# Row dots with the mask term as their seed, single-row matmuls and a mask in five parts, in a recommender's attention kernel

## The reference, cut to what matters

```python
maskf = hist_mask.astype(dt)
decay = jnp.exp(-(softplus(decay_alpha) + 1e-6) * hist_age_hours) * maskf
mean_hist = (hist_items * maskf[..., None]).sum(1) / (maskf.sum(1, keepdims=True) + 1e-06)
q = mean_hist @ Wq.T
k, v = hist_items @ Wk.T, hist_items @ Wv.T                 # (512, 200, 128)
scores = einsum('bd,btd->bt', q, k) * scale + jnp.log(decay + 1e-12)
scores = jnp.where(hist_mask, scores, -jnp.inf)
attn = softmax(scores); long_term = einsum('bt,btd->bd', attn, v)
# short_term: mean of five items; g: sigmoid gate of mean popularity and age
user = g * short_term + (1 - g) * long_term
out = layernorm(user) * ln_gamma + ln_beta                  # (512, 128)
```

## Time and profile before

| | |
|---|---|
| time, median of 3 runs | 208.8 us (206.55 to 209.44) |
| time of the profiled execution | 206.09 us |
| its span, first to last instruction | 204.4 us |
| mean granted TensorE clock | 0.946 |
| busy: TensorE, VectorE, ScalarE, GpSimd | 168.8, 174.1, 118.8, 143.0 us |
| moved from and to memory | 55.19 MB, 270 GB/s |

### The profile page before, as it was taken

One profiled execution on the slowest core, in us unless ns is written; L12 is line 12 of the kernel. 1 busy time (PEld: TensorE's weight loads), 2 busy tenths in 40 slices (PEclk: granted clock), 3 DMA queues, 4 the chain that ended last, 5 costly groups with the idle time before them and its releaser, 6 DMA issues.

```text
span 204.4 us, 6882 instructions
## 1 busy us (share of the span) xinstructions
PE 168.8 (83%) x2005; PEld 102.9 (50%) x2005; DVE 174.1 (85%) x1332; ACT 118.8 (58%) x646; POOL 143.0 (70%) x167
## 2 busy tenths in 40 slices
PE   0172864887999699899999999999999999997890
PEld 0132432444565456565655565656565656564570
DVE  0513989989999999999899999898999998989703
ACT  2002255587767377667676777676677776768410
POOL 3467982488959587777869887769698877486311
PEclk9998555699999999999999999999999999999998
DMA  7949969996888878988988899988888998600000
GB/s 36 303 153 304 257 223 420 418 431 287 311 293 326 325 268 287 339 328 277 333 311 331 345 330 338 321 318 323 311 328 287 386 363 313 246 2 14 0 3 13
DMA packets 15683, 55.19 MB, mean 270 GB/s; under 512 B 10160, under 2 KB 11312, under 8 KB 11568
## 3 DMA queue, kind: packets, MB, share of 16 engines
q1 hardware_dynamic: 15088, 53.64, 74.2%
q0 software_dynamic: 576, 1.33, 2.2%
HBM read 54.70 MB, written 0.26 MB: 269 GB/s over the span
## 4 chain that ended last, share of the span: by engine, by line
POOL 31%; issue 25%; PE 17%; DVE 14%; DMA 8%; ACT 3%; POOLq 1%; ACTq 0%; SPq 0%; DVEq 0%
POOL gprod L286 14%; DVE junk_v L686 9%; PE ps_sum L358 6%; POOL mblk L266 6%; DMA x<-in_r_hist_items_dram 5%; POOL pblk L275 5%; PE ps_wx L358 4%; DMA mask_p<-in_r_hist_mask_dram 3%; PE ps_sum L368 3%; PE ps_query L377 2%; POOL pop_taken L344 2%; POOL age_taken L344 2%; ACT sums L467 1%; POOL taken L322 1%; PE ps_group L386 1%
## 5 line engine op out<-in xcount | busy, mean ns | idle before, releaser
L686 DVE SCALAR_TENSOR_TENSOR junk_v<-x,ps_query 128x128 f32<-128x128 f32 x576 | 127.2, 277 | 7.5 <-ACT query L485 7.3
L286 POOL TENSOR_TENSOR gprod<-x,query 128x512 f32<-128x512 f32 x64 | 71.9, 1144 | 32.0 <-ACT query L485 31.9
L458 ACT ACTIVATE gprod<-gprod 128x128 f32<-128x128 f32 x224 | 66.1, 299 | 2.7 <-DVE kept L653 1.4
L358 PE MATMUL ps_wx<-x,pblk 128*32 128x256 f32 (+1 forms) x832 | 67.2, 380 | 0.0
L358 PE MATMUL ps_sum<-x,mblk 128*32 128x256 f32 (+1 forms) x832 | 63.5, 404 | 3.2 <-DMA x<-in_r_hist_items_dram 3.1
L358 PEld LDWEIGHTS ps_sum<-x,mblk 128*32 128x32 f32 (+1 forms) x832 | 34.2, 115 | 25.0 <-issue 7.0
L686 DVE DVE_READ_ACCUMULATOR junk_v<-x,ps_query 128x1 f32 x576 | 45.9, 80 | 0.0
L458 ACT ACTIVATION_READ_ACCUMULATOR gprod<-gprod 128x1 f32 x224 | 42.7, 190 | 0.0
L467 ACT ACTIVATE sums<-ps_sum,rcnt_rows 128x256 f32<-128x256 f32 x32 | 15.1, 472 | 29.9 <-PE ps_sum L358 29.9
L275 POOL TENSOR_TENSOR pblk<-own,ex 128x400 f32<-128x400 f32 x32 | 27.4, 875 | 6.1 <-ACT ex L493 6.1
L358 PEld LDWEIGHTS ps_wx<-x,pblk 128*32 128x32 f32 (+1 forms) x832 | 25.0, 107 | 12.6
(11 more groups left out here) (94 smaller groups left out, 100.4 us busy)
## 6 DMA issues: line engine op xcount, KB each, us to landing
x<-in_r_hist_items_dram SPq DMA_DIRECT2D x32, 1600.0 KB, 8.8
age_p<-in_r_hist_age_hours_dram SPq DMA_DIRECT2D x1, 400.0 KB, 14.6
out_dram<-y SPq DMA_DIRECT2D x4, 64.0 KB, 4.2
mask_p<-in_r_hist_mask_dram SPq DMA_DIRECT2D x1, 100.0 KB, 6.1
mask_u<-in_r_hist_mask_dram SPq DMA_DIRECT2D x1, 100.0 KB, 3.5
wq<-in_L_rec_Wq_dram SPq DMA_DIRECT2D x1, 64.0 KB, 5.7
wk<-in_L_rec_Wk_dram SPq DMA_DIRECT2D x1, 64.0 KB, 3.8
wv<-in_L_rec_Wv_dram SPq DMA_DIRECT2D x1, 64.0 KB, 3.7
```

The lines of the kernel that those rows point to most:

```text
L286: nc.gpsimd.tensor_tensor(gprod[:, t, a * D:b * D].rearrange("p (r d) -> p r d", d=D), rows((k % GP) * PAIR + t, r0 + a, r0 + b), query[:, ...
L358: ins = nc.tensor.matmul(dst[c:c + n * TU, 0:n * D], blk[:, k % 2, t, 2 * m:2 * m + n, :].rearrange("p r u -> p (r u)"), x[:, i + t, 2 * m ...
L458: ins = nc.scalar.activation(src, src, ACT.Copy, accum_out=score[:, k % 2, t, DOTS + r:DOTS + r + 1])
L686: ins = V.scalar_tensor_tensor(out=junk_v[:, t, r, :], in0=x[:, (k % GP) * PAIR + t, r * D:(r + 1) * D], scalar=1.0, in1=c_query[t], op0=A ...
```

## The change

1. Dots: `tensor_tensor_reduce` takes the place of `scalar_tensor_tensor`. Its sum starts from a seed in SBUF, the column of `hide` for that tile and row, and it writes straight into `kept`. ScalarE's rows are 129 elements long: GpSimd copies the seven columns of `hide` into `gprod` behind the products. `mask_scores` is gone, and `kept` has two buffers.
2. TensorE takes single rows: 25 matmuls of 16 weight columns and 128 moving columns for each sum in place of 13 of 32 and 256. `fold` is one matmul, and the copies of sums are 128 wide.
3. No loop on any engine: all steps are straight code.
4. The mask and the ages come in five parts (of 4, 4, 8, 8 and 8 tiles), each with its own conversion, counts, `hide` and logarithm; the decay's floor is the bias of the logarithm. The first tile of items is the third load, the small loads stand later, and tile 3 no longer waits for the gathers. Four PSUM banks are cleared once.

```diff
-CUT_SUMS, CUT_MEAN = 4, 8
+CUTS = ((7, 15), (3, 11))
+SUM_COL, WX_COL = (0, 0), (1, 1)
+PARTS = ((0, 4), (4, 8), (8, 16), (16, 24), (24, 32))
+PART_LOADS = {3: 2, 6: 3, 10: 4}
@@ SyncE
+            load_mask(0)
             sp.dma_start(mask_u[:, :, :], mask_n).then_inc(ld_mask_u, 16)
             load(0, 0, 0)
+            for dst, src in ((wq, Wq), (wk, Wk)):
+                sp.dma_start(dst[:, :], src).then_inc(ld_weights, 16)
+            sp.dma_start(da[:, :], decay_alpha.unsqueeze(0).broadcast_to([P, 1])).then_inc(ld_alpha, 16)
+            load_age(0)
+            load(0, 0, 1)
+            load_mask(1)
+            load_age(1)
+            load(1, 1, 0)
+            load(1, 1, 1)
...
-            load(1, 1, 0)
-            sp.wait_ge(last_gathered, 2 * NGROUP * 16)
-            load(1, 1, 1)
@@ GpSimd, products
+                nc.gpsimd.tensor_copy(gprod[:, t, :, D], hide[:, at + DOTS:at + ROWS]).then_inc(gprod_ready, 1)
                 for a, b in GCHUNKS:
-                    nc.gpsimd.tensor_tensor(gprod[:, t, a * D:b * D].rearrange("p (r d) -> p r d", d=D),
+                    nc.gpsimd.tensor_tensor(gprod[:, t, a:b, 0:D],
@@ TensorE
-                for m in ms:
-                    n = min(2, ROWS - 2 * m)
-                    c = 32 * (m % CG)
-                    ins = nc.tensor.matmul(dst[c:c + n * TU, 0:n * D],
-                                           blk[:, k % 2, t, 2 * m:2 * m + n, :].rearrange("p r u -> p (r u)"),
-                                           x[:, i + t, 2 * m * D:(2 * m + n) * D],
+                for m in range(a, b):
+                    c = 32 * ((m + col) % CG)
+                    ins = nc.tensor.matmul(dst[c:c + TU, 0:D], blk[:, k % 2, t, m, :], x[:, i + t, m * D:(m + 1) * D],
...
-                for rr in range(2):
-                    ins = nc.tensor.matmul(c_mean[t], sums[:, t, rr * D:(rr + 1) * D], fold[:, rr, :],
-                                           start=(rr == 0), stop=(rr == 1))
+                nc.tensor.matmul(c_mean[t], sums[:, t, :], fold[:, :], start=True, stop=True).then_inc(mean_done, 1)
@@ ScalarE
-                    src = gprod[:, t, r * D:(r + 1) * D]
+                    src = gprod[:, t, r, :]
                     ins = nc.scalar.activation(src, src, ACT.Copy,
-                                               accum_out=score[:, k % 2, t, DOTS + r:DOTS + r + 1])
+                                               accum_out=kept[:, k % 2, t, DOTS + r:DOTS + r + 1])
...
-                nc.scalar.activation(sums[:, t, :], ps_sum[t][:, 0:2 * D], ACT.Copy,
+                nc.scalar.activation(sums[:, t, :], ps_sum[t][:, 0:D], ACT.Copy,
...
+                nc.scalar.activation(decay[:, a:b], decay[:, a:b], ACT.Ln, bias=tiny[:, :]).then_inc(decay_ln, 1)
@@ VectorE
-            def mask_scores(s, k):
...
-                V.tensor_tensor(kept[:, :, 0:ROWS], score[:, k % 2, :, :],
-                                hide[:, bass.ds(s * PROWS, PROWS)].rearrange("p (t r) -> p t r", t=PAIR), ALU.add).then_inc(kept_ready, 1)
@@ VectorE, dots
                 if a == 0:
+                    if t == 0 and has(s, 2):
+                        dve.wait_ge(exp_done, (s - 1) * PAIR)
                     dve.wait_ge(query_ready, s * PAIR + t + 1)
                 for r in range(a, b):
-                    ins = V.scalar_tensor_tensor(out=junk_v[:, t, r, :], in0=x[:, (k % GP) * PAIR + t, r * D:(r + 1) * D],
-                                                 scalar=1.0, in1=c_query[t], op0=ALU.mult, op1=ALU.mult,
-                                                 accum_out=score[:, k % 2, t, r:r + 1])
+                    at = (s * PAIR + t) * ROWS + r
+                    ins = V.tensor_tensor_reduce(out=junk_v[:, t, r, :], in0=x[:, (k % GP) * PAIR + t, r * D:(r + 1) * D],
+                                                 in1=c_query[t], scale=1.0, scalar=hide[:, at:at + 1], op0=ALU.mult,
+                                                 op1=ALU.add, accum_out=kept[:, k % 2, t, r:r + 1])
@@ VectorE, step
+                for n in parts_from(s + 1):
+                    setup_mask(n)
+                    setup_hide(n)
+                for n in parts_from(s):
+                    setup_inverse_counts(n)
+                    setup_log_decay(n)
```

More of the change, by code:

```diff
@@ L186, in build, with steps, parts_from @@
         block = ctx.enter_context(nc.Block())
[L188 to L196, removed]
+        def steps(step, last_step, first=0):
+            for s in range(first, last_step + 1):
                 step(s // GP, s % GP)
         def has(s, back, n=NPAIR):
-            return not isinstance(s, int) or 0 <= s - back < n
+            return 0 <= s - back < n
+        def parts_from(s):
+            return [n for n, (a, b) in enumerate(PARTS) if n and a == s * PAIR]
         def rows(i, a, b):
@@ L339, in step, with gather_context @@
                     inverse_deviation(g - 1)
-            pool.wait_ge(rows_ready, 1)
-            for q in range(NGROUP):
+            def gather_context(q):
                 for dst, src in ((pop_taken, pop_rows), (age_taken, age_rows)):
@@ L421, in step @@
                     if has(s, back):
-                        weighted_sums(s - back, k - back, u, range(CUT_SUMS, CUT_MEAN))
+                        weighted_sums(s - back, k - back, u, cut_sums, cut_mean)
                     if has(s, 0):
@@ L524, in step @@
                     copy_weighted(s - 2, 0)
+                for n in parts_from(s + 2):
+                    log_decay(n)
+                if s == 2:
+                    act.wait_ge(gate_in, 1)
+                    nc.scalar.activation(st[:, 12:14, :], st[:, 10:12, :], ACT.Exp).then_inc(gate_exp, 1)
             nc.scalar.preload_act_table_set("natural_log_exp_and_others")
@@ L777, in step @@
                         dots(s, k, 0, i, i + 1)
+            for unused in ps_sum + ps_wx:
+                link(V.memset(unused[:, 0:D], 0.0))
+            assert made[0] == DVE_BANKS
+            V.memset(tiny[:, :], TINY).then_inc(tiny_ready, 1)
             link(V.memset(pmax[:, :], 0.0))
-            link(V.memset(kept[:, :, ROWS:ROWS + 1], FLOOR))
-            setup_early()
-            setup_decay()
-            step(0, 0)
-            setup_hide()
-            step(0, 1)
-            step(0, 2)
-            setup_last_weights()
-            steps(dve, step, NPAIR + 3, first=3)
+            link(V.memset(kept[:, :, :, ROWS:ROWS + 1], FLOOR))
+            setup_mask(0)
+            setup_hide(0)
+            setup_inverse_counts(0)
+            setup_first_rows()
+            setup_wqk()
+            setup_alpha()
+            setup_log_decay(0)
+            steps(step, NPAIR + 3)
     return nc
```

262 lines of the change are left out of this document (153 added, 109 removed).

## The result

The changed kernel takes 228.5 us in the median (228.1 to 229.2); the kernel before, run on the same chip beside it, 207.9 us. The ratio is 1.103 (95% interval 1.097 to 1.109): the change costs 10%. The profiled execution took 229.15 us, with a span of 227.4.

What follows compares the result with a forecast made beforehand. VectorE was taken as the bound, TensorE close behind. From the profiled 206.1 us, +34.6 - 5.6 - 4.0 + 0 + 0 - 3.8 + 0 - 0.8 gave 226.5, forecast as 227 us; range 203 to 247.

Steps and rivals of the forecast that it cites:

- rival 1: VectorE's dots: the seed's fetch is hidden while the dot ahead streams, pointer price 0, total 196 us; chance 0.13.
- The dots' pointer, +34.6: VectorE's 576 dots: reading the seed through a pointer adds 60 ns to each, +34.6 us (0 to +46).
- rival 2: VectorE's dots: the separate accumulator read goes and the seed's price stays, total 205 us; chance 0.09.
- `mask_scores`, -5.6: VectorE: 16 masking instructions go, at 0.35 us each, -5.6 us (-4 to -6.8).
- TensorE, -4: TensorE's single rows and halved folds: they can give only VectorE's waits for queries, -4 us (0 to -5.2).
- Rival 3: TensorE can't issue single rows fast enough, 62 ns a record, total 244 us; chance 0.12.
- Straight code, 0: All engines: three jumps of a loop go, costed at 0 (-1 to +3 us).
- The start, -3.8: Start of the kernel: items load third, first dot at 15.6 instead of 19.36 us, -3.8 us (0 to -6).
- Rival 4: Start: ScalarE waits for an age part behind items, start gives 0, total 230 us; chance inside the forecast's 0.61.
- Parts and floor, 0: VectorE: five parts instead of one cost +1.5 us, the floor's pass goes, -1.5: 0 (-1 to +3).
- The end, -0.8: After the last dot: the masking and half of the last eight folds leave, -0.8 us (0 to -1.5).

Runs made afterwards that it cites:

- e1_const_seed: The changed kernel with the constant 0.0 as the dots' seed instead of the pointer into `hide`, so rows 0 to 17 go unmasked: 202.1 us, ratio 0.973.
- e3_before_pointer: The kernel before, with its old dots reading their constant 1.0 through a pointer to a column of ones: 230.5 us, ratio 1.111.
- e2_plain_dots: The changed kernel with the old dots (constant 1.0), VectorE then adding `hide` to its 36 scores of a pair: 207.2 us, ratio 0.998.
- e10_single_straight: The kernel before with TensorE's single rows, one fold and narrower copies, and its loop written out as straight code: 202.0 us, ratio 0.984.
- e9_before_straight: The kernel before with its loop written out as straight code, nothing else: 206.8 us, ratio 0.998.
- e7_before_single_rows: The kernel before with the change's TensorE part alone (single rows, one fold, 128-wide copies), still with the loop: 219.1 us, ratio 1.060.
- e5_two_parts: e2_plain_dots with two parts of mask and ages (tiles 0 to 3 and 4 to 31) instead of five: 205.7 us, ratio 0.995.
- e8_before_pool_mask: The kernel before with `mask_scores` moved from VectorE to GpSimd, still with the loop: 221.0 us, ratio 1.066.

## Why the prediction was right

The forecast was 227 and the time 228.5, and the reason given for it holds. That they lie so near is in part luck, since two errors cancelled. By the forecast's own rival 1 a kernel without the pointer would have taken 196 us, so that the pointer was put at 30.5 us of the total and all the rest at a gain of 10.1. The runs show 26.4 for the pointer (e1_const_seed against the changed kernel; 23.0 in e3_before_pointer) and 5.4 for the rest (e1_const_seed against the kernel before). The first error is that VectorE's time isn't all on the total: its waits, and what its other operations take, change with the room that the dots leave. The second is the term of the parts, below.

- *The dots' pointer, +34.6.* Right as VectorE's time: 60 ns were measured between dots (0.268 for 0.208 us in the longest runs of them). Rival 1 (the fetch hides behind the dot ahead) and rival 2 (the separate read goes) are refuted by rows of after: 0.27 us apart, and a `DVE_READ_ACCUMULATOR2_ANT` behind each dot. The rule of the Trainium skill that spoke against this term (Vector Engine (DVE) Microarchitecture Reference, section 5.2) holds for the new instruction with a constant: the dots come 0.208 us apart, as the estimate from it had said. It doesn't hold with a pointer.
- *`mask_scores`, -5.6.* Near. From tile 8 on, twelve of them took 3.6 us from their start to the next start in the kernel before, 0.30 each and not 0.35. But the edit can't be had without the pointer: when e2_plain_dots gave the addition back, it took 9.7 us, not 6.8.
- *TensorE, -4.* The waits for queries went from 7.3 to 4.2 us, so -3.1 in the changed kernel, and to 0 from tile 8 on. But e3_before_pointer has the same without single rows (2.0 us in all, 0 from tile 8 on): the slower dots alone do it. With quick dots, in e10_single_straight against e9_before_straight, single rows give 4.8 us (202.0 for 206.8).
- *Rival 3, that TensorE can't issue single rows.* Refuted by a row of after: 78 records in 2.58 us, 33 ns each, where the bound assumed 62.

```profile
202.91 2.58 PE L392 MATMUL ps_wx<-x,pblk 128*16 128x128 f32 x78
```

  The rule of the Trainium skill that gave 62 ns for each matmul (TensorE: Matmul & The Clock Gate, section "Wait — 56ns, not 53.3ns?") doesn't describe this stretch; its floor of about 25 ns isn't contradicted by that mean.
- *Straight code, 0.* Right by itself (e9_before_straight, 0.998). The working missed that it is a condition of the single rows: with the loop they cost 12 us (e7_before_single_rows).
- *The start, -3.8.* Right in time: first dot at 15.43 for a forecast of 15.6. Rival 4 falls. One reading in its working is not in the rows: that the first sums of the kernel before ran at the lower clock level. The granted clock of 11.8 to 15.2 us is given as 1.00; what speaks for the lower level is the pace alone, 26 records in 3.20 us where the earlier trace rows has 52 in 3.21.
- *Parts and floor, 0.* This term failed, and by VectorE's timeline it is where most of the missing gain went, in two places. The set-up of a part takes 2.0 to 2.3 us of VectorE in each of the three rounds that have one, while VectorE is never idle there; the three passes over the whole mask had taken 5.7 us in the kernel before, but in gaps in which the next query wasn't there. And the prediction didn't look where `setup_gate` went: from such a gap to between tiles 3 and 4, 7.2 us with the copy ahead of it. Neither was shown by a run. e5_two_parts took the set-up out of the rounds, and the total stayed the same within the noise. In it `setup_gate` took 3.6 us only, and tiles 0 to 3 were no shorter (30.8 us for 30.4 in e2_plain_dots), as VectorE waited 7.2 us for queries in them; a kernel with `setup_gate` put back wasn't run. e2_plain_dots and e10_single_straight agree with the reading: the first has its first dot 4.5 us earlier (17.61 for 22.12) and starts tile 8 3.4 us later (71.69 for 68.28).
- *The end, -0.8.* -1.8: 13.5 us from the last dot's start to the end of the span, where it was 15.2.

Expected and seen of the profile after: dots of 337 ns (335 to 345 forecast) 0.27 us apart; no L653; but a round of 49 us and not 45 to 46, and waits for queries of 4.2 us and not under 3. The forecast round left out the part's set-up, 2.3 us in each of the two. The instructions of `short_term` are longer (L708 833 ns for 663 before), but from start to next start the five of a round take what they took, 3.3 to 3.5 us.

## What to carry to other kernels

A per-partition pointer as the scalar of a VectorE instruction had the same price in each of the 576 issues here. Issued 576 times to save 16 instructions, it paid 35 us of VectorE's time, 23 to 26 of the total, to save some 5: count issues, not passes. Where set-up work is moved or cut in parts, ask of each piece what VectorE was waiting for at the old place, and what GpSimd does at the new one. And where code is added to a loop, look at the instruction queues' packets inside it: if they appear where there were none, write the loop out before judging the edit.

## What the runs showed of the hardware

- The pointer costs 60 ns between instructions of 128 elements, in `scalar_tensor_tensor` and in `tensor_tensor_reduce`; the latter costs nothing else over the former, and has its own separate read of 79 ns.
- With more instructions in the loop, packets of instructions move in its later rounds (15 for 0 in e7_before_single_rows, 9 for 2 in e8_before_pool_mask), and stalls stand behind the jump: 5.2 and 4.5 us on TensorE in the first, up to 4.4 us on VectorE in the second, 12 and 14 us in the total. Without the loop they are gone.
- Two small VectorE operations that met a GpSimd `tensor_tensor` ended within 0.05 us of it: 0.92 us for 0.18, and 0.93 for 0.16, in the rows above.
- In four column strips TensorE ran 78 single-row fp32 records at 33 ns each.
